# Last feed-forward unit reordered with up pieces ahead of down pieces, and block 3's routing moved behind the down products of an expert turn

## The reference

```python
x = x + _L0_xattn_ref(_layernorm(x, axis=-1), ctx_1024, ...)
x = x + _L0_ffn_ref(_layernorm(x, axis=-1), wg, w1, w3, w2)
# inside the first:
y = layernorm(y + attention(y, y, y, causal=True), g1, beta1)
y = layernorm(y + attention(y, Z, Z, causal=False), g2, beta2)   # Z has 1601 rows
h = jax.nn.relu(jnp.einsum('bsd,df->bsf', y, w1) + b1)           # 256 -> 1024
y = layernorm(y + jnp.einsum('bsf,fd->bsd', h, w2) + b2, g3, beta3)
# inside the second:
probs = jax.nn.softmax(x @ wg.T, axis=-1)
topk_w, topk_idx = jax.lax.top_k(probs, 2)          # weights made to sum to 1
y = jnp.einsum('tei,ehi->teh', jax.nn.silu(h1) * h3, w2)   # 256 -> 512 -> 256 per expert
out = jnp.einsum('te,teh->th', expert_w, y)
```

## Time and profile before

| | |
|---|---|
| median of 3 runs | 534.37 us (532.86 to 537.04) |
| the profiled execution's own time | 529.8 us |
| its span, first to last instruction | 527.9 us |
| mean granted TensorE clock | 0.994 |
| PE busy | 497.2 us (94%) |
| DVE, ACT, POOL busy | 377.3, 286.2, 287.9 us |

### The profile page before, as it was taken

How to read it: one execution, slowest core, us unless ns; L and a number is a source line. 1 busy time by engine, 2 the same in 40 slices (tenths; PEclk the granted TensorE clock), 3 DMA queues, 4 the chain that set the end, 5 groups by cost and what they waited for, 6 DMA issues and landing times.

```text
span 527.9 us, 10992 instructions
## 1 busy us (share of the span) xinstructions
PE 497.2 (94%) x3686; PEld 325.3 (62%) x3686; DVE 377.3 (71%) x968; ACT 286.2 (54%) x575; POOL 287.9 (55%) x324
## 2 busy tenths in 40 slices
PE   7899999999899999898999999899999799999992
...
DMA packets 135314, 65.61 MB, mean 124 GB/s; under 512 B 109757, under 2 KB 126590, under 8 KB 135262
## 3 DMA queue, kind: packets, MB, share of 16 engines
...
...
## 4 chain that ended last, share of the span: by engine, by line
PE 61%; DVE 13%; POOL 8%; ACT 6%; DMA 6%; issue 3%; SPq 1%; POOLq 0%; ACTq 0%; DVEq 0%
PE ps L1203 50%; PE ps L1298 3%; DMA probT<-prob 3%; PE ps L1300 2%; PE ps L1299 2%; DVE cmax L1740 2%; PE ps L1529 2%; ACT ps L1013 1%; DMA y<-hrow,qst 1%; POOL nrm L783 1%; ACT prob L1012 1%; POOL tT L891 1%; POOL y L840 1%; ACT tT L999 1%; DVE prob L1881 1%
## 5 line engine op out<-in xcount | busy, mean ns | idle before, releaser
L1203 PE MATMUL ps<-arena,probT 128*128 128x256 f16 (+2 forms) x1092 | 180.0, 318 | 4.8 <-DMA probT<-prob 2.4
L1203 PEld LDWEIGHTS ps<-arena,probT 128*128 128x128 f16 (+1 forms) x1092 | 104.6, 97 | 62.0 <-issue 9.2
L964 POOL DMA_INDIRECT out<-y,qst x39 | 62.5, 1602 | 17.9 <-DMA out<-y,qst 9.4
L1203 PE MATMUL ps<-arena,qT 128*128 128x512 f16 (+1 forms) x384 | 68.9, 332 | 1.6 <-DVE prob L1881 1.2
L2299 DVE SCALAR_TENSOR_TENSOR ps<-ps,w1m 128x512 f32<-128x512 f32 x39 | 27.3, 699 | 57.1 <-ACT w1m L1142 54.4
L1012 ACT ACTIVATE prob<-ps,nbias 128x512 f16<-128x512 f32 x64 | 38.9, 609 | 53.3 <-DVE nbias L1746 53.3
L1142 ACT ACTIVATE w1m<-ps 128x512 f32<-128x512 f32 x39 | 23.3, 597 | 77.6 <-PE ps L1203 62.9
L1203 PE MATMUL ps<-arena,tT 128*128 x468 | 57.4, 273 | 0.7 <-DVE tT L2400 0.6
L779 POOL TENSOR_TENSOR rstd<-veps,expo 128x1 f32<-128x1 f32 x16 | 9.6, 599 | 88.3 <-DVE veps L1775 88.3
L1203 PEld LDWEIGHTS ps<-arena,qT 128*128 128x128 f16 x384 | 32.4, 97 | 37.1 <-issue 3.2
L938 POOL DMA_INDIRECT y<-hrow,qst x39 | 40.1, 1028 | 19.8 <-issue 9.9
...
## 6 DMA issues: line engine op xcount, KB each, us to landing
...
```

The costliest lines, as they stand in the source:

```text
L964: g.indirect_dma_start(out[:rows_of(p), :], bass.IndirectOffsetOnAxis(ridx[:, n:n + 1], 0), ys[:, n % RING, :], None, compute_op=ALU.add). ...
L1203: r = t.matmul(o, lhs(a), rhs(b), start=first and n == 0, stop=last and n == 2)
```

## The change

PE, last unit: `make_lists(0)` goes ahead of `up(3, 6)` (it stood behind), `x_trans(0)` ahead of `down(3, 6)` and `x_trans(1)` ahead of `down(3, 7)` (both stood behind the last down). The pieces of `rest` are sorted so that up pieces come first (8 of the 13), and `e_ups(0)` waits for these 8; the wait for all 13 stands in turn 3.

PE, expert turns: block 3's transposes, logits and ranks, and the products of lists 1 and 2, go behind `e_downs` of a turn, in the bank pair `psT`, and one turn earlier (`H_AT, LOGITS_AT, RANKS_AT` 9, 10, 11; list 1 in turn 6, list 2 in turn 14). The second half of the transposes stays between `e_ups` and `x_trans`.

POOL: the first product of the last tile's norm moves to DVE (`last_norm`); `out_adds(2)` goes behind `gather(1)`; `rstd_of("m_", 3)` ahead of `add(3)`; block 3's `gates` and `weigh` one turn earlier; gather 17 one turn earlier.

ACT: `out_scaled(2)` goes from chunk 2 to chunk 6 of the last unit, the table load for silu behind the first two `x_copy`, `silu(0)` ahead of `h_hi(2)`, block 3's `h_hi` and `h_copy` behind `weighted` of their turn.

DVE: the last unit's low halves `hid_lo` go ahead of block 2's norm work, the tables of list 0 are spread between them, and five of the low halves of `rest` go further back.

```diff
-GATHERS_FROM = {1: 4, 2: 11}
+GATHERS_FROM = {1: 4, 2: 10}
...
-        rest = [n for n in rest if n >= in_zT] + [n for n in rest if n < in_zT]
-        R_ZT = NE * NP - in_zT
+        rest = sorted(rest, key=lambda n: (n % NP >= 2 * KD, n < in_zT))
+        R_ZT = [n < in_zT for n in rest].index(True)
+        R_UPS = [n % NP >= 2 * KD for n in rest].index(True)
         REST_AT = {2: {5: (0,), 6: (1, 2), 7: (3,)},
-                   3: {0: (4,), 1: (5,), 2: (6,), 3: (7, 8), 4: (9,), 5: (10,), 6: (11,), 7: (12,)}}
+                   3: {0: (4,), 1: (5,), 2: (6,), 3: (7,), 4: (8,), 5: (9, 10), 7: (11, 12)}}
...
-        H_AT, LOGITS_AT, RANKS_AT = 10, 11, 12
-        LISTS_AT = {7: 1, RANKS_AT + 3: 2}
+        H_AT, LOGITS_AT, RANKS_AT = 9, 10, 11
+        LISTS_AT = {6: 1, RANKS_AT + 3: 2}
...
-            return 2 - 2 * (n % 2)
+        def behind(n):
+
+            return psT[n % 2]
...
-            return psO[half] if j == 2 else ps[spare(H_AT) + half]
+            if j == 2:
+                return psO[half]
+            return ps[3 - 2 * ((H_AT + 1) % 2)] if half else behind(H_AT)
...
             def ln_affine(pre, i, q, row):
-                pool.wait_ge(sm[pre + "rstd"], i + 1)
-                g.tensor_scalar(nrm[:, q, :], u[:, q, :], mv[:, q, 0:1], rstd[:, q, :], ALU.subtract,
-                                ALU.mult).then_inc(sm[pre + "nrm"], 1)
+                if i < NT - 1:
+                    pool.wait_ge(sm[pre + "rstd"], i + 1)
+                    g.tensor_scalar(nrm[:, q, :], u[:, q, :], mv[:, q, 0:1], rstd[:, q, :], ALU.subtract,
+                                    ALU.mult).then_inc(sm[pre + "nrm"], 1)
                 pool.wait_ge(sm[pre + "nrm"], i + 1)
                 g.tensor_tensor(nrm[:, q, :], nrm[:, q, :], vec[:, row, :], ALU.mult).then_inc(sm[pre + "gam"], 1)
                 pool.wait_ge(sm[pre + "gam"], i + 1)
...
-            out_adds(2)
...
             gather(0)
             gather(1)
+            out_adds(2)
             rstd_of("m_", 2)
...
                     if n and issued < min(NJ, n + AHEAD) and n >= GATHERS_FROM.get(phase_of(issued), 0):
                         gather(issued)
                         issued += 1
+                if n == 4:
+                    rstd_of("m_", NB - 1)
                 if n:
                     add(n - 1)
-                if n == 4:
-                    rstd_of("m_", NB - 1)
...
-                    if u == NB - 1 and f == 2:
+                    if u == NB - 1 and f == 6:
                         out_scaled(2)
...
-            a.activation(shift[:], shift[:], ACT.Silu)
...
             x_copy(0, 0)
             x_copy(1, 1)
+            a.activation(shift[:], shift[:], ACT.Silu)
+            silu(0, 0)
             h_hi(2)
-            silu(0, 0)
...
-                if n == H_AT:
-                    h_copy(NB - 1, 0)
-                if n == H_AT - 1:
-                    h_hi(NB - 1)
                 act_hi(n, n % RING)
                 if BEHIND <= n < ACT_END:
                     weighted(n - BEHIND, (n - BEHIND) % RING)
+                if n == H_AT - 1:
+                    h_hi(NB - 1)
+                if n == H_AT:
+                    h_copy(NB - 1, 0)
...
             down(3, 2)
             up(3, 5)
             down(3, 3)
+            make_lists(0)
             up(3, 6)
-            make_lists(0)
             down(3, 4)
             up(3, 7)
             down(3, 5)
+            wait(pe, "f_lo", KF * NB - 2)
+            x_trans(0, 0)
             down(3, 6)
+            wait(pe, "f_lo", KF * NB - 1)
+            x_trans(1, 1)
             wait(pe, "r_tab", 1)
             expert_of(0)
             down(3, 7)
-            wait(pe, "f_lo", KF * NB - 2)
-            x_trans(0, 0)
-            wait(pe, "f_lo", KF * NB - 1)
-            x_trans(1, 1)
             wait(pe, "f_lo", KF * NB)
-            wait(pe, "st_lo", G_FF + len(rest))
+            wait(pe, "st_lo", G_FF + R_UPS)
             wait(pe, "e_xcp", 2)
             e_ups(0, 0)
             wait(pe, "n_u", NT)
...
+                if n == H_AT + 2:
+                    wait(pe, "h_half", 1)
                 e_ups(n, q)
-                if between:
+                if n == 2:
+                    wait(pe, "e_alo", 2)
+                    logits(2)
+                if n == H_AT + 1:
                     wait(pe, "e_alo", n)
-                    between()
+                    h_trans(NB - 1, 1)
+                    wait(pe, "h_cp", 3)
+                if n == LOGITS_AT + 1:
+                    wait(pe, "r_lg", NB)
+                if n == RANKS_AT + 1:
+                    routing_read(NB - 1)
+                if n - 1 in LISTS_AT:
+                    wait(pe, "r_list", LISTS_AT[n - 1] + 1)
                 if nxt:
                     x_trans(n + 1, (s + 1) % RING)
                 if n == BEHIND + 1:
                     routing_read(2)
                 if n == BEHIND:
                     wait(pe, "r_lg", NB - 1)
+                    wait(pe, "st_lo", G_FF + len(rest))
                 if n >= BEHIND:
                     e_downs(n - BEHIND, (n - BEHIND) % RING)
                 if n == BEHIND:
                     ranks(2)
                     counts(1)
+                if n == H_AT:
+                    h_trans(NB - 1, 0)
+                if n == LOGITS_AT:
+                    logits(NB - 1)
+                if n == RANKS_AT:
+                    ranks(NB - 1)
+                    counts(2)
+                if n in LISTS_AT:
+                    make_lists(LISTS_AT[n])
...
+            def last_norm():
+
+                wait(dve, "c_y", NT - 1)
+                wait(dve, "c_rstd", NT)
+                v.tensor_scalar(nrm[:, 1, :], u[:, 1, :], mv[:, 1, 0:1], rstd[:, 1, :], ALU.subtract,
+                                ALU.mult).then_inc(sm["c_nrm"], 1)
...
             hid_lo(2, 5)
             split_chunk(split_lo, dve, 2, 5)
             rest_los(2, 5)
+            last_norm()
             table_starts(0)
             hid_lo(2, 6)
             hid_lo(2, 7)
             rest_los(2, 6)
             y_lo(NB - 1)
             rest_los(2, 7)
-            table_keys(0)
             for m in range(TB):
                 out_tile(2, m)
+            for m in range(TB - 1):
+                out_stats(2, m)
             hid_lo(3, 0)
-            for m in range(TB):
-                out_stats(2, m)
+            out_stats(2, TB - 1)
             out_moments(2)
             hid_lo(3, 1)
+            table_keys(0)
+            hid_lo(3, 2)
             table_experts(0)
-            rest_los(3, 0)
-            hid_lo(3, 2)
-            centre(2, range(TB))
+            hid_lo(3, 3)
             rows_hot(1)
-            hid_lo(3, 3)
+            hid_lo(3, 4)
             tiles_hot(0)
             spread_vals(0)
-            rest_los(3, 1)
-            hid_lo(3, 4)
-            rest_los(3, 2)
-            rest_los(3, 3)
+            centre(2, (0, 1))
             hid_lo(3, 5)
             list_read(0)
-            rest_los(3, 4)
+            centre(2, (2, 3))
+            rest_lo(dve, 4)
+            rest_lo(dve, 5)
+            rest_lo(dve, 6)
             hid_lo(3, 6)
-            rest_los(3, 5)
+            rest_lo(dve, 7)
+            rest_lo(dve, 8)
             hid_lo(3, 7)
+            rest_lo(dve, 9)
             for m in range(TB):
                 x1_stats(2, m)
             x1_aggr(2)
-            rest_los(3, 6)
-            rest_los(3, 7)
             for m in range(TB):
                 out_tile(NB - 1, m)
+            rest_lo(dve, 10)
             h_norm(2)
             table_rest(0)
-            h_lo(2)
...
             j = NB - 1
             gated(0, 0)
+            h_lo(2)
             act_lo(0, 0)
+            rest_lo(dve, 11)
             gated(1, 1)
             for m in range(TB):
                 out_stats(j, m)
             act_lo(1, 1)
             out_moments(j)
+            rest_lo(dve, 12)
...
+                if n == 7:
+                    first_out(j)
+                if n == H_AT + 1:
                     wait(dve, "h_tr", 4)
...
+                if n == 12:
+                    table_keys(2)
+                if n == 13:
+                    spread_vals(2, (1,))
...
+                    list_read(1)
+                    table_experts(1)
                     centre(j, (2, 3))
-                    table_experts(1)
                 if n == 7:
-                    first_out(j)
...
+                    h_lo(j)
```

62 lines of the change are left out of this document (19 added, 43 removed).

## The result

The changed kernel took 538.19 us (median of 20 runs, 530.91 to 1051.71; without the one run of 1051.71 the highest is 545.41), the kernel before 532.97 (20 runs, 529.61 to 537.04). The ratio is 1.0066, with a 95% interval of 1.0039 to 1.0094: slower, by under 1%. The profiled execution took 537.89 us, its span 536.1.

What follows compares the result with a forecast made beforehand. PE's own work was taken to bound the expert turns, after 8.4 us of holds; PE would lead by 4.1 us, of which 3.4 arrive through the adds: 534.4 - 3.4 = 531.0 us, range 527.3 to 535.2.

Steps and rivals of the forecast that it cites:

- a lead that would partly arrive: At the kernel's end: of PE's 4.1 us lead 2.9 to 3.4 arrive through the adds; 3.4 taken.
- Last unit: Up to the experts' start on PE: holds go, leads of 0.45, then 1.9, then 3.9 us at `e_ups(0)`.
- What takes this back: Start of the experts: block 2's adds, now behind gather 1, take 4.0 us and delay gather 2; PE stands 4 us.
- the lead of 3.9 is gone, to 0: PE behind `e_ups(0)`: the hold on gather 2 uses up the lead, with ends of 1.0 to -1.1 us.
- Turns 2 to 16: PE's expert turns: holds for gather 9 and list 2 go, block 3's is 1.5; PE 4.1 us earlier.
- The adds: POOL's chain of adds: add 3 at 381.8, gates hidden in a 3.78 us gap, a lead of 2.1 us by add 10.
- rival 2: Add chain: gates hide behind nothing, add 3's lateness of 1.7 to 2.7 us stays; up to 1.4 late, about 535.6; chance 0.12.
- The prediction's own sign of being wrong: At the end: the last add more than 1.5 us away from where PE's last product moved.
- Turns 17 on are not held, since a gather has 2.5 us or more to land.: PE's late expert turns: no holds, as a weighted result waits for the add four before and gathers have 2.5 us.

Runs made afterwards that it cites:

- e3: The kernel before with only the last unit's part of the change, expert turns as before: ratio 1.0067, median +3.5 us against the kernel before.
- e5: The changed kernel with gather 2 ahead of block 2's adds and block 3's power behind add 3 again: ratio 0.9997 to the kernel before, median +0.3 us.
- e16: The changed kernel with one edit, gather 17 moved behind add 9 on POOL: ratio 1.0059 to the kernel before, median +3.9 us.
- e15: The changed kernel with gather 2 ahead of block 2's adds, the power behind add 3, gather 17 behind add 9: ratio 0.9970 to the kernel before.
- e8: The changed kernel with 12 unread matmuls on PE where it stood still ahead of the third x_trans: ratio 1.0094 to the kernel before, median +5.2 us.
- e7: The changed kernel with two low halves (pieces 8, 9) moved on DVE behind block 2's norm statistics: ratio 0.9992 to the kernel before, median +2.7 us.
- e9: The changed kernel with gather 2 ahead of block 2's adds, the power behind add 3, low halves 8 and 9 behind block 2's statistics: ratio 1.0032.
- e6: The kernel before with one POOL edit, block 3's power ahead of add 3 instead of behind it: ratio 1.0008, median +1.0 us.

## Why the prediction was wrong, point by point

I forecast 531.0 and a lead that would partly arrive; measured were 538.2, outside the range, and the sign was the other one.

- **Last unit.** Right in the middle: relative to `y_trans`, `down(3, 3)` was forecast at 15.25 and went at 15.2, gather 1 at 20.45 and 20.6. The hold ahead of `y_trans` did not go (0.57, now for `hid_lo(2, 6)`). `e_ups(0)` was forecast at 25.25 and went at 26.84: most of the missing 1.6 is the 1.40 on `hid_lo(3, 7)` behind DVE's stall.
- **What takes this back.** The mechanism was right: the adds of block 2 behind gather 1, a hold on gather 2. The step that failed is "the lead of 3.9 is gone, to 0". I gave the contention to POOL (4.0 us of adds beside undisturbed low halves); it fell on DVE. Gather 2 went at 29.3 behind `y_trans` against 29.15 forecast, the transposes of its rows came 0.9 later than forecast, and then came a term that stood nowhere in the sum: the clock behind a hold of 3.2 us, 1.7 us. `x_trans(3)`, at 35.1 before, was at 38.2: not a lead of 0, but 3.1 late. The sum itself held 0.6 of that, counted from `y_trans` (gather 2's transposes at 31.95, before 31.4); 0.9 is the later landing, and the rest the slow product.
- **Turns 2 to 16.** The holds for gather 9, list 2 and its expert number went, block 3's was 1.72 against 1.5 forecast: the sizes were right. PE's `x_trans(17)` was 0.8 us earlier than before instead of the 4.1 forecast for turn 16: about what the start lost (3.1). (The terms given for turns 11 to 16 add up to 414.9, not 415.1.)
- **The adds.** This is where the sign turned. Add 3 was forecast 66.55 behind `y_trans` and went at 68.7, add 10 at 102.75 and 106.2: instead of 2.1 us of lead, 1.9 of lateness against the kernel before (104.4). The gates did hide in part, as forecast (adds 6 to 8 took 11.9 us, before 14.0). This is rival 2 with more lateness than its price, and it got 0.12. The prediction's own sign of being wrong was there: against the kernel before, PE's last product moved by 3.8 us and the last add by 7.6.
- **"Turns 17 on are not held, since a gather has 2.5 us or more to land."** False: PE stood at five gathers (0.18 to 1.38 us) in turns 18 to 22, where each gather is queued between two late adds, and from `x_trans(17)` to `x_trans(38)` it took 4.9 us longer than before (91.7 against 86.9). I had let the adds limit only the end, and not PE through the gathers.
- The cause as far as shown. The last unit's part alone loses as much as the whole change, there through PE's late start (e3). In the changed kernel the turns' part wins PE's lateness back, and the two POOL edits together, gather 2 ahead of block 2's adds and the power behind add 3, take the loss away, in two pairs of kernels (changed to e5, e16 to e15). Making PE early at the start without them recovers nothing (e8). That the adds are the way from these two edits to the time rests on the rows of the changed kernel and of e8, each of one execution.
- Open: why either edit alone recovers next to nothing by the ratio; why e7's ratio is as low as e5's and e9's is not; why e6 cost less than its 2.5 us; and why in the late turns of the changed kernel an add landed 4.6 to 4.8 us after its start (adds 11 to 14 go 4.9 to 5.1 us apart) where in the kernel before most go 4.2 us apart.
